# One attention and mixture-of-experts layer on one core: late expert splits moved among the first tiles

## The chip, the cores and the metric

The kernel runs on one core of one Trainium2 chip. The metric is the device time of one execution in microseconds (us); less is better. The core has five engines that work at once and meet by semaphores: TensorE (PE; its weight loads are listed apart as PEld), VectorE (DVE), ScalarE (ACT), GpSimd (POOL) and SyncE (SP), which here only issues DMA. Every engine works through its own instructions in order.

## What is computed

The input `x` is 2 batches of 1024 tokens of 256 numbers. It is normalised (`xn`), and the output is `x + attention(xn) + experts(xn)`, all in float32.

```python
# attention: 16 heads, 4 key/value heads; a semantic part of 32 and a rotated part of 32 per head
k2, v2 = pool(k), pool(v)     # tokens 0..895: means over 14 blocks of 64; tokens 896..1023: as they are
scores = (q_sem @ k_sem2.T + q_geo @ k_geo2.T) / sqrt(32) * exp(logit_scale)
out = softmax(where(k_pos <= pos, scores, NEG_INF)) @ v2 @ Wo
# experts: 16, the best 4 of each token, hidden width 224
g, u = xn @ gate_proj[e], xn @ up_proj[e]
y = sum over the token's 4 experts of top_w * ((silu(g) * u) @ down_proj[e])
```

## The kernel before, in words

The 2048 tokens are 8 tiles of 128 in each of 2 batches (`u`, `b` = 0, 1; tile `t` = 0..7). Only tile 7 sees single keys beside the block means, so its attention is written apart.

**Opening.** `x` is loaded, normalised and turned (`xT`). TensorE projects the rotated keys and the router's logits; VectorE ranks them and takes the best four (L1009 to L1060), and works out the slot of each of the 8192 pairs of token and expert in a list sorted by expert. VectorE also rotates keys (`rope_k`, L991), takes the weights of the four choices one choice at a time (`weights(r)`, L1061), writes the block means of `xn`, the head scales (`hscale`, L1039), and the plan of the tasks (`plan_tasks`, L1102): a task is 128 rows of the sorted list with one expert, `NS` = 79 tasks in all, `tasks` per expert.

**Sending.** GpSimd scatters the rows of `xn` to the list in memory, `xn_by_expert`, in 16 rounds of 4 indirect DMAs (L709 to L720); every round waits until that before it has landed. In the last four rounds it also takes the low parts of experts 4 and 5.

**Splits.** An expert's weights (3 transfers of 224 KB, `load_expert`, L393) are held as a high and a low part, so that three fast products give float32's precision. The high part is two copies on ScalarE (`split_high`, L814: 0.94 and 0.62 us), the low part two subtractions on VectorE (L1192: 1.08 and 0.69 us) or on GpSimd (L687: some 2.1 and 1.3 us). The semaphore `w_hi` counts experts with a high part and `w_lo` those with both, in order, so that each low part waits for the one before it. Experts 0 to 3 (`EARLY` = 4) are loaded in the opening. The others are loaded in groups, `LATE`, with one semaphore a group. SyncE issues group 0 before the loop over blockwise tiles (L615), groups 1 to 3 in turns `i` = 0, 1, 2 of it and groups 4 and 5 later (L623 to L631), group 6 after the first eight tasks (L648). Each turn `i` first stores the sum of tile `i` (`store_sum(i)`, which waits until VectorE has added it, `c_out` >= i + 2), then loads a residual (`load_residual(i + 2)`, which waits until the store before it into that buffer has landed), then the weights.

**Local attention** (tile 7): eight units of one batch and one key/value head. TensorE scores (`l_score`), VectorE takes maxima, ScalarE exponentiates, VectorE divides, TensorE turns (`l_turn`) and multiplies by values (`l_value`); `beside(n)` adds to unit `n` other work: the folded values (`rep_values`, `fold_values`), the tables of the tasks, the first low parts. `l_attend` and `l_attend_blocks` then give the output of tile 7.

**Blockwise attention** (tiles 0 to 6, `attention_pe`, `attention`, `attention_act`). For tile `t` TensorE turns the queries of both batches; then for each batch it projects the queries of tile `t + 1` and scores tile `t`; after the first batch's scores it turns the probabilities of tile `t - 1` (`p_turn`); after both it multiplies those by values (`attend`, L1610), for which it waits for ScalarE's copy of the turned probabilities (`c_pT`). ScalarE in tile `t`: the copies of the queries, the high parts of `SPLITS[t]`'s first expert with their wait, then the copies `p_keep` for tile `t - 1` and the exponentials of tile `t`:

```python
high = SPLITS[t.number]
for k in high[:1]:
    split_late(k)          # waits for w_late of k's group
if not t.first:
    for u in range(NB):
        p_keep(u, t.more(-1))
```

`SPLITS` is written by hand: experts 4, 5 in tile 1; 6, 7 in tile 3; 8, 9 in tile 4; 10 in tile 5. `HEAD` = (11, 12) follows before the first tile of the experts, and `IN_LOOP` = 13: experts 13 to 15 are split in steps 5 to 7 (high) and 6 to 8 (low, on VectorE) of the tiles.

**Tiles of the experts.** 79 tasks, in a software pipeline (`step`): in step `j` TensorE turns the rows of task `j + 2`, multiplies task `j + 1` by gate and up (`three`, six products), turns the activations of task `j` and multiplies those of task `j - 1` by down; ScalarE and VectorE do for each product the copies and subtractions that split it. GpSimd scatters each result into the output, adding to what is there (L741), and begins when its low parts of experts 6 to 12 are done (L723). ScalarE's copy of result `n` waits for scatter `n - 4`. Rows come by `load_task` into 8 slots: SyncE issues tasks 0 to 3 when the rows are sent and tile 6 is scored (L637 to L643), then two stores (the second waits for tile 6's sum), tasks 4 to 7, `load_late(6)`, and then task `j + 8` for each `j`. Steps -2 to 8 are written out, the rest is a loop of 8 steps.

Of the kernel before, what the change touches and what calls it, by code (L numbers as in the profile page):

```python
# [36 lines left out]
P = 128  # L37
# [34 lines left out]
LATE = ((4, 5), (6, 7), (8, 9), (10, 11), (12,), (13,), (14, 15))  # L72
# [20 lines left out]
def build(nc, x, wq_sem, wk_sem, wq_geo, wk_geo, wv, wo, logit_scale, router_w, expert_bias, gate, up, down,  # L93
# [9 lines left out]
    with ctx:  # L103
# [379 lines left out]
        ROUND = 8  # L483

# [48 lines left out]
        def steps(eng, step, rounds, carry=None):  # L533
# [4 lines left out]
            for r in range(-2, ROUND + 1):  # L538
                step(Tile(0, r))
            if carry:  # L540
                carry()
            with eng.Fori(1, rounds) as i:
# [3 lines left out]
                if carry:  # L546
                    carry()
# [5 lines left out]
        def _(sp):  # L553
# [50 lines left out]
            by_batch = vw_d.rearrange("(b r) d -> r b d", b=NB)  # L604
            sp.dma_start(vw[:, :, 0, :], by_batch[0:P, :, :]).then_inc(vw_in, DMA)
# [11 lines left out]
            def load_behind(n, t):  # L617

                for u in range(NB):
                    sp.wait_ge(c_s[u], t)  # L620
                load_late(n)
# [26 lines left out]
            load_late(6)  # L648
# [17 lines left out]
        def _(gp):  # L666
            nc.gpsimd.memset(zero[:, :], 0.0).then_inc(zeros_ready, 1)
            nc.gpsimd.memset(logit[:, :, E:EX], -FAR).then_inc(sentinels_ready, 1)
# [85 lines left out]
        def _(act):  # L754
# [37 lines left out]

            act.wait_ge(pooled, REMOTE)
# [17 lines left out]
            act.wait_ge(vloc_done, 1)  # L811
            nc.scalar.copy(vloc[:, :, :], bank[VLOC_BANK][:, :].rearrange("p (b n) -> p b n", b=NB)).then_inc(vloc_kept, 1)

            def split_high(e):  # L814
                nc.scalar.copy(of_expert(wgu_h, e), of_expert(wgu, e))  # L815
                nc.scalar.copy(of_expert(wdn_h, e), of_expert(wdn, e)).then_inc(w_hi, 1)
# [58 lines left out]
            def split_late(k):  # L875
                if k == SENT:
                    for p in range(GT):
                        act.wait_ge(xs_in[p], K * GROUPS * DMA)
                for n, ks in enumerate(LATE):
# [924 lines left out]
```

## Time and profile before

| | us |
|---|---|
| median of 3 runs (lowest, highest) | 395.76 (393.83, 397.96) |
| the profiled execution, its own time | 395.17 |
| its span, first to last instruction | 393.4 |
| PE busy | 350.6 (89%) |
| DVE busy | 242.4 (62%) |
| POOL busy | 232.0 (59%) |
| ACT busy | 182.6 (46%) |
| mean granted TensorE clock | 0.953 |

The profiled execution took 1.8 us more than its span. Times inside it are us from the span's start. Its stages, by TensorE's work: opening to 59, local attention to 111, blockwise attention to 176, tiles to 384. A granted clock of 1.00 is 2.4 GHz, 0.50 is 1.2 GHz.

### The profile page before, as it was taken

To read this page: it belongs to the slowest core of one execution; us is meant where nothing else is said; L and a number is where in the kernel's file an instruction comes from. 1 tells how busy PE (TensorE), PEld (TensorE's weight loads), DVE (VectorE), ACT (ScalarE), POOL (GpSimd) and SP (SyncE) were. 2 spreads that over 40 slices of the span, in tenths; PEclk is the share of its full clock that TensorE was granted. 3 is DMA by queue.
4 is the path that set the end of the run, shared out by engine and by line. 5 is a ranking of instruction groups with operands and counts; after the bars stand their busy time and mean duration, and the time that the engine had idled before them with its cause. 6 is when DMAs were issued, how large, how long until landed. Compare 5 with 4: busy or idle time off the path is not lost.

```text
span 393.4 us, 8217 instructions
## 1 busy us (share of the span) xinstructions
PE 350.6 (89%) x2085; PEld 287.6 (73%) x2086; DVE 242.4 (62%) x784; ACT 182.6 (46%) x530; POOL 232.0 (59%) x207
## 2 busy tenths in 40 slices
PE   0498997998979999987977999999999999999991
PEld 0393675645746677666876999999999999999881
DVE  3879996488458789852547455555555555555550
ACT  1540186458013344444455455555555555555550
POOL 0600456546664464659987466666666666666664
PEclk9998998699989999996998899999999999999996
DMA  7993112224146388863686476666776766666544
GB/s 247 361 314 89 55 60 84 75 80 125 69 147 209 114 257 257 248 213 86 174 176 100 71 113 107 112 107 107 110 113 108 111 112 112 109 108 107 70 52 53
DMA packets 50094, 52.33 MB, mean 133 GB/s; under 512 B 5632, under 2 KB 47120, under 8 KB 50072
## 3 DMA queue, kind: packets, MB, share of 16 engines
q0 software_dynamic: 14640, 19.34, 29.8%
q1 hardware_dynamic: 35432, 32.73, 29.1%
q8 instruction: 10, 0.16, 0.2%
q14 instruction: 12, 0.10, 0.1%
HBM read 30.14 MB, written 21.91 MB: 132 GB/s over the span
## 4 chain that ended last, share of the span: by engine, by line
PE 48%; DMA 18%; POOL 14%; issue 9%; DVE 6%; ACT 2%; POOLq 1%; SPq 1%; DVEq 0%; ACTq 0%
PE bank L1366 39%; DMA xn_by_expert<-x_all,slot_i 14%; POOL xn_by_expert L714 13%; PE bank L1728 4%; PE bank L1704 4%; DMA out_rows<-y,idx 2%; DMA x_all<-in_L_attn_x 1%; ACT x_all L763 1%; POOL wgu_lo L691 1%; DVE stats L954 1%; PE bank L1378 1%; DVE logit_left L1024 1%; DMA xg<-xn_by_expert 1%; POOLq L103 0%; ACT wgu_hi L815 0%
## 5 line engine op out<-in xcount | busy, mean ns | idle before, releaser
L741 POOL DMA_INDIRECT out_rows<-y,idx x79 | 124.5, 1576 | 66.3 <-ACT y L930 39.6
L714 POOL DMA_INDIRECT xn_by_expert<-x_all,slot_i x64 | 66.2, 1034 | 55.6 <-DMA xn_by_expert<-x_all,slot_i 33.7
L1366 PE MATMUL bank<-wgu_hi,xh 128*128 x158 | 65.9, 417 | 4.7 <-DVE wdn_lo L1195 2.6
L1346 DVE SCALAR_TENSOR_TENSOR act<-bank,xg,sg 128x224 f32<-128x224 f32 x79 | 35.6, 451 | 55.7 <-ACT sg L917 55.7
L1366 PE MATMUL bank<-wgu_lo,xh 128*128 x158 | 59.3, 375 | 0.0
L1366 PE MATMUL bank<-wgu_hi,xl 128*128 x158 | 58.8, 372 | 0.0
L917 ACT ACTIVATE sg<-bank 128x224 f32<-128x224 f32 x79 | 28.3, 358 | 62.3 <-PE bank L1366 62.3
L1338 DVE TENSOR_TENSOR xl<-bank,xh 128x256 fp32r<-128x256 f32 x79 | 33.5, 425 | 35.5 <-ACT xh L908 35.5
L1366 PE MATMUL bank<-wdn_hi,ah 112*128 x158 | 51.8, 328 | 0.6 <-issue 0.5
L1366 PE MATMUL bank<-wdn_hi,al 112*128 x158 | 44.8, 283 | 0.0
L1366 PE MATMUL bank<-wdn_lo,ah 112*128 x158 | 44.6, 282 | 0.0
L930 ACT COPY y<-bank 128x256 f32<-128x256 f32 x79 | 29.5, 374 | 30.6 <-PE bank L1366 27.4
L1366 PEld LDWEIGHTS bank<-wgu_hi,xh 128*128 128x128 f32 x158 | 30.4, 192 | 7.3 <-issue 5.2
L1704 PE MATMUL bank<-const_k,xg 128*128 128x128 f32 x158 | 31.2, 279 | 4.6 <-DMA xg<-xn_by_expert 4.6
L908 ACT CAST xh<-bank 128x256 fp32r<-128x256 f32 x79 | 29.8, 378 | 7.4 <-PE bank L1704 7.0
L1354 DVE TENSOR_TENSOR al<-bank,ah 112x256 fp32r<-112x256 f32 x79 | 32.8, 415 | 0.5 <-ACT ah L921 0.5
L1366 PEld LDWEIGHTS bank<-wgu_hi,xl 128*128 128x128 f32 x158 | 30.4, 192 | 2.8
L1366 PE MATMUL bank<-wqg,xT 128*128 128x512 f32 x64 | 32.1, 628 | 0.0
L1366 PEld LDWEIGHTS bank<-wgu_lo,xh 128*128 128x128 f32 x158 | 30.6, 194 | 1.2
L1366 PEld LDWEIGHTS bank<-wdn_hi,ah 112*128 112x128 f32 x158 | 30.3, 192 | 1.2 <-issue 1.0
L1728 PE MATMUL bank<-const_k,act 128*112 128x128 f32 x158 | 30.6, 275 | 0.0
L1366 PEld LDWEIGHTS bank<-wdn_lo,ah 112*128 112x128 f32 x158 | 30.4, 193 | 0.0
(235 smaller groups left out, 658.2 us busy)
## 6 DMA issues: line engine op xcount, KB each, us to landing
xg<-xn_by_expert SPq DMA_DIRECT2D x79, 129.0 KB, 2.5
wgu<-in_L_ffn_gate_proj SPq DMA_DIRECT2D x16, 224.0 KB, 4.0
wgu<-in_L_ffn_up_proj SPq DMA_DIRECT2D x16, 224.0 KB, 4.6
wdn<-in_L_ffn_down_proj SPq DMA_DIRECT2D x16, 224.0 KB, 4.9
x_all<-in_L_attn_x SPq DMA_DIRECT2D x8, 256.0 KB, 5.0
xr<-in_L_attn_x SPq DMA_DIRECT2D x14, 128.0 KB, 2.2
out_rows<-xr SPq DMA_DIRECT2D x14, 128.0 KB, 3.8
out_rows<-y,idx POOLq DMA_INDIRECT x79, 3.8
```

Of the source, the lines that this page charges most:

```text
L691: nc.gpsimd.tensor_tensor(of_expert(wgu_l, e), of_expert(wgu, e), of_expert(wgu_h, e).bitcast(F32), ALU.subtract)
L714: gp.indirect_dma_start(xs_d, bass.IndirectOffsetOnAxis(slot_i[:, z, r:r + 1], 0), x_all[:, z, :], None).then_inc(xs_in[p], DMA)
L741: gp.indirect_dma_start(out_rows, bass.IndirectOffsetOnAxis(idx[r % RING][:, 0:1], 0), ysb[r % 4][:, :], None, compute_op=ALU.add).then_in ...
L908: nc.scalar.copy(xh[t.par][:, :, :], bank[t.par][:, 0:D].rearrange("p (c n) -> p c n", c=DC)).then_inc(xh_ready, 1)
L917: nc.scalar.activation(sg[t.par][:, :], bank[2 + t.par][:, 0:I], ACT.Silu).then_inc(sg_ready, 1)
L930: nc.scalar.copy(ysb[t.place][:, :], bank[6 + t.par][:, 0:D]).then_inc(y_ready, 1)
L1338: nc.vector.tensor_tensor(xl[t.par][:, :, :], bank[t.par][:, 0:D].rearrange("p (c n) -> p c n", c=DC), xh[t.par][:, :, :].bitcast(F32), AL ...
L1346: nc.vector.scalar_tensor_tensor(av[t.par][:, :], bank[2 + t.par][:, I:2 * I], xg[t.slot][:, D + 1:D + 2], sg[t.par][:, :], ALU.mult, ALU. ...
L1354: nc.vector.tensor_tensor(al[t.par][:, :, :], bank[4 + t.par][0:IH, 0:2 * P].rearrange("p (c n) -> p c n", c=2), ah[t.par][:, :, :].bitcas ...
L1366: return nc.tensor.matmul(o, lhsT, rhs, start=start, stop=stop)
L1704: last = nc.tensor.transpose(bank[t.par][:, c * P:(c + 1) * P], xg[t.slot][:, c * P:(c + 1) * P], ident)
L1728: last = nc.tensor.transpose(bank[4 + t.par][0:IH, c * P:(c + 1) * P], av[t.par][:, c * IH:(c + 1) * IH], ident)
```

## The change

Constants and the order of the splits. Groups 4 and 5 of one expert each become one of two; ScalarE has experts 4 and 5 in tile 1, 6 and 7 in tile 3, 8 and 9 in tile 5 of the attention, none ahead of the tiles, and 10 to 15 in steps 2 to 13 of the tiles, one of an expert's two copies in each step; VectorE has their low parts in steps 4 to 15, one subtraction in each. GpSimd's loop ends with expert 9. Steps -2 to 16 of the tiles are written out (`HEAD = 2 * ROUND`), and the loop has one turn less.

```diff
-LATE = ((4, 5), (6, 7), (8, 9), (10, 11), (12,), (13,), (14, 15))
+LATE = ((4, 5), (6, 7), (8, 9), (10, 11), (12, 13), (14, 15))
-        SPLITS = ((), (4, 5), (), (6, 7), (8, 9), (10,), ())
-        HEAD = (11, 12)
+        SPLITS = ((), (4, 5), (), (6, 7), (), (8, 9), ())
-        IN_LOOP = 13
+        IN_LOOP = 10
+        HIGH_FROM, LOW_FROM = 2, 4
...
         def _(act):
...
                     for u in range(NB):
                         p_keep(u, Pair(0, REMOTE - 1))
-                    for k in HEAD:
-                        split_late(k)
...
-                if j.counts is None and j.r in (5, 6, 7):
-                    split_late(IN_LOOP + j.r - 5)
+                n = j.r - HIGH_FROM
+                if j.counts is None and 0 <= n < 2 * (E - IN_LOOP):
+                    split_late(IN_LOOP + n // 2, (n % 2,))
...
         def _(dve):
...
-                if j.counts is None and j.r in (6, 7, 8):
-                    k = IN_LOOP + j.r - 6
-                    dve.wait_ge(w_lo, k)
-                    split_low(k)
+                n = j.r - LOW_FROM
+                if j.counts is None and 0 <= n < 2 * (E - IN_LOOP):
+                    k = IN_LOOP + n // 2
+                    if n % 2 == 0:
+                        dve.wait_ge(w_lo, k)
+                    split_low_part(k, n % 2)
```

SyncE's loads: groups 1 and 2 in turns 1 and 3, group 3 after tasks 0 to 3, groups 4 and 5 after tasks 4 to 7.

```diff
             for i in range(REMOTE - 3):
                 store_sum(i)
                 load_residual(i + 2)
-                if i < 3:
-                    load_late(i + 1)
-                else:
-                    load_behind(4, 2)
+                if i % 2:
+                    load_late(i // 2 + 1)
             store_sum(REMOTE - 3)
-            load_behind(5, 4)
...
             for j in range(RING // 2):
                 load_task(j, j)
+            load_late(3)
             for i in range(REMOTE - 2, REMOTE):
                 store_sum(i)
             for j in range(RING // 2, RING):
                 load_task(j, j)
-            load_late(6)
+            load_late(4)
+            load_late(5)
```

A task for every expert, in `plan_tasks`:

```diff
                 link(nc.vector.tensor_tensor(tasks[:, :], tiles_f[:, :], bound[:, 1, :], ALU.subtract))
+                link(nc.vector.tensor_scalar(tasks[:, :], tasks[:, :], 1.0, None, ALU.max))
```

Opening and local attention. On VectorE the four operations that make the weights' sums and the three of the head scales move behind the rotation of keys 2 and 3 and the slots (the scales behind all keys), the fold of the block means (`x_fold`) in front of `weights(1)`, and `weights(2)` and `weights(3)` into units 2 and 6 of the local attention. On TensorE the local values (`vloc`, from `xT[REMOTE]` now) come right after the rotated queries of tile 7, and ScalarE's copy of them ahead of its others; the folded values come before the first turn:

```diff
             l_score(0)
             l_score(1)
+            rep_values()
             for n in range(UNITS):
                 l_turn(n)
...
             l_attend(0)
             l_value(UNITS - 1)
-            q_project(0, Pair(0, 0))
+            for u in range(NB):
+                q_project(u, Pair(0, 0))
...
             turn_probabilities(1)
-            q_project(1, Pair(0, 0))
             l_attend_blocks(1)
```

VectorE accordingly does `rope(u, Pair(0, 0))` for both batches, then `split_low(3)` and `keep_before()`, then `l_attended(u)`, each followed by a new `memset` of `prT[u]`.

128 rows in the values' products: `attend` takes all 128 rows of every chunk in place of the 32 to 128 that hold probabilities. The new memset of `prT`, and one of `vw[:, :, 1, :]` on GpSimd at the start, make the rest zero.

```diff
-                parts = [(prT[u][0:rest, n, :], vw[0:rest, u, n, :]) for n, (at, rest) in enumerate(t.chunks)]
+                parts = [(prT[u][:, n, :], vw[:, u, n, :]) for n in range(len(t.chunks))]
```

## Rows read from the trace of the kernel before

**Rows 1.** Windows of ten us: busy (x instructions) by engine, granted clock, DMA share, GB/s.
```profile
70.00:80.00 10.00, 10.00 (x43) 5.43 (x44) 6.07 (x26) 4.55 (x13) 4.67 (x6) 0.68 0.18 64
...
150.00:160.00 10.00, 10.00 (x54) 7.05 (x53) 9.00 (x27) 5.39 (x12) 4.64 (x6) 1.00 0.83 255
...
250.00:260.00 10.00, 10.00 (x70) 9.28 (x69) 5.65 (x19) 5.20 (x17) 6.50 (x5) 1.00 0.69 112
```

**Rows 2.** The chain that ended last, where the tiles begin: start, us, what.
```profile
170.33 5.13 DMA xn_by_expert<-x_all,slot_i
177.71 2.11 DMA xg<-xn_by_expert
```

**Rows 3.** Timeline of ScalarE (ACT), blockwise attention: start, us, engine, line, operation [idle before <-releaser].
```profile
144.48 0.94 ACT L815 CAST wgu_hi<-wgu 128x896 fp32r<-128x896 f32 x1 [2.22 <-DMA wdn<-in_L_ffn_down_proj]
...
154.20 0.94 ACT L815 CAST wgu_hi<-wgu 128x896 fp32r<-128x896 f32 x1 [3.48 <-DMA wdn<-in_L_ffn_down_proj]
...
155.56 0.42 ACT L872 COPY prT<-bank 128x128 f32<-128x128 f32 x2
...
163.88 0.94 ACT L815 CAST wgu_hi<-wgu 128x896 fp32r<-128x896 f32 x1 [4.73 <-DMA wdn<-in_L_ffn_down_proj]
```

**Rows 4.** Timeline of SyncE's DMA issues, blockwise attention.
```profile
131.66 1.47 SPq L588 DMA_DIRECT2D out_rows<-xr  x2
135.51 1.03 SPq L583 DMA_DIRECT2D xr<-in_L_attn_x  x2
...
141.47 0.89 SPq L588 DMA_DIRECT2D out_rows<-xr  x2
145.47 0.81 SPq L583 DMA_DIRECT2D xr<-in_L_attn_x  x2
146.33 0.43 SPq L400 DMA_DIRECT2D wgu<-in_L_ffn_gate_proj  x1
```

**Rows 5.** Timeline of TensorE (PE), blockwise attention and the first transpose of the tiles.
```profile
147.83 1.11 PE L1366 MATMUL bank<-vw,prT 96*128 96x256 f32 x4
...
165.71 2.58 PE L1366 MATMUL bank<-vw,prT 128*128 128x256 f32 x8 [0.38 <-ACT prT L872]
...
178.72 0.66 PE L1704 MATMUL bank<-const_k,xg 128*128 128x128 f32 x2 [3.19 <-DMA xg<-xn_by_expert]
```

**Rows 6.** Timeline of TensorE, local attention and the change to blockwise.
```profile
64.49 0.66 PE L1506 MATMUL bank<-const_k,lex 128*128 128x128 f32 x4 [2.06 <-DVE lex L1184]
...
66.81 3.62 PE L1366 MATMUL bank<-x_fold,wv_rep 128*128 128x30 f32 x16
...
113.98 3.53 PE L1366 MATMUL bank<-wqg,xT 128*128 128x512 f32 x4
```

**Rows 7.** Timeline of TensorE, the first gate product of five of the tiles.
```profile
191.71 0.46 PE L1366 MATMUL bank<-wgu_hi,xh 128*128 x1
...
206.06 0.74 PE L1366 MATMUL bank<-wgu_hi,xh 128*128 x1 [2.18 <-DVE xl L1338]
...
215.18 0.47 PE L1366 MATMUL bank<-wgu_hi,xh 128*128 x1 [2.56 <-DVE wdn_lo L1195]
...
221.52 0.45 PE L1366 MATMUL bank<-wgu_hi,xh 128*128 x1
...
223.91 0.45 PE L1366 MATMUL bank<-wgu_hi,xh 128*128 x1
```

**Rows 8.** Timeline of ScalarE, fifth step of the tiles.
```profile
203.34 0.37 ACT L930 COPY y<-bank 128x256 f32<-128x256 f32 x1 [2.33 <-DMA out_rows<-y,idx]
```

**Rows 9.** Timeline of GpSimd (POOL), its first output scatter.
```profile
199.20 1.62 POOL L741 DMA_INDIRECT out_rows<-y,idx  x1 [0.16 <-issue]
```

**Rows 10.** Timeline of SyncE's DMA issues, first tiles.
```profile
191.70 0.44 SPq L400 DMA_DIRECT2D wgu<-in_L_ffn_gate_proj  x1
...
195.84 4.35 SPq L635 DMA_DIRECT2D xg<-xn_by_expert  x4
```

**Rows 11.** Tile `xg`, 186 to 206 us: time to landing.
```profile
DMA to landing us min/median/max: 2.1/2.6/4.4
```

More of the change, by code:

```diff
@@ L483, in build @@
         ROUND = 8
+        HEAD = 2 * ROUND
         class Tile:
@@ L533, in steps @@
         def steps(eng, step, rounds, carry=None):
-            for r in range(-2, ROUND + 1):
+            for r in range(-2, HEAD + 1):
                 step(Tile(0, r))
             if carry:
-                carry()
-            with eng.Fori(1, rounds) as i:
+                carry(HEAD)
+            with eng.Fori(HEAD // ROUND, rounds) as i:
                 counts = Counts(eng, ROUND, i), Counts(eng, ROUND // 4, i, True), Counts(eng, ROUND // RING, i, True)
@@ L810, in _, with split_high_part @@
                 keep_rep(n)
-            act.wait_ge(vloc_done, 1)
-            nc.scalar.copy(vloc[:, :, :], bank[VLOC_BANK][:, :].rearrange("p (b n) -> p b n", b=NB)).then_inc(vloc_kept, 1)
+            def split_high_part(e, part):
+                if part == 0:
+                    nc.scalar.copy(of_expert(wgu_h, e), of_expert(wgu, e))
+                else:
+                    nc.scalar.copy(of_expert(wdn_h, e), of_expert(wdn, e)).then_inc(w_hi, 1)
             def split_high(e):
-                nc.scalar.copy(of_expert(wgu_h, e), of_expert(wgu, e))
-                nc.scalar.copy(of_expert(wdn_h, e), of_expert(wdn, e)).then_inc(w_hi, 1)
+                for part in range(2):
+                    split_high_part(e, part)
             def l_exp(n):
@@ L873, in p_keep, with split_late @@
                 last.then_inc(c_pT[u], 1)
[L875 to L879, printed above, removed]
-                    if k == ks[0]:
-                        act.wait_ge(w_late[n], len(ks) * 3 * DMA)
-                split_high(k)
+            def split_late(k, parts=(0, 1)):
+                if 0 in parts:
+                    if k == SENT:
+                        for p in range(GT):
+                            act.wait_ge(xs_in[p], K * GROUPS * DMA)
+                    for n, ks in enumerate(LATE):
+                        if k == ks[0]:
+                            act.wait_ge(w_late[n], len(ks) * 3 * DMA)
+                for part in parts:
+                    split_high_part(k, part)
             def attention_act(t):
@@ L1329, in _ @@
             for u in range(NB):
+                rope(u, Pair(0, 0))
+            split_low(3)
+            keep_before()
+            for u in range(NB):
                 l_attended(u)
-                rope(u, Pair(0, 0))
+                link(nc.vector.memset(prT[u][:, :, :], 0.0))
             pairs(attention)
@@ L1438, in _ @@
                 last.then_inc(l_q, 1)
+            pe.wait_ge(kv_in, 4 * DMA)
+            pe.wait_ge(slots_ready, 1)
+            for b in range(NB):
+                for c in range(DC):
+                    last = mm(bank[VLOC_BANK][:, b * D:(b + 1) * D], xT[REMOTE][:, b, c, :], wv_s[:, c, :], c == 0, c == DC - 1)
+            last.then_inc(vloc_done, 1)
             for t in range(4, REMOTE):
@@ L1473, in _ @@
                 rep_keys(n)
-            pe.wait_ge(slots_ready, 1)
-            for b in range(NB):
-                for c in range(DC):
-                    last = mm(bank[VLOC_BANK][:, b * D:(b + 1) * D], x_keys[:, c, b, NBLK:NKEY], wv_s[:, c, :], c == 0, c == DC - 1)
-            last.then_inc(vloc_done, 1)
             def l_score(n):
@@ L1543, in beside @@
                 if n == 0:
-                    rep_values()
                     pe.wait_ge(starts_ready, 1)
@@ L1645, in _ @@
             l_value(UNITS - 1)
-            q_project(0, Pair(0, 0))
+            for u in range(NB):
+                q_project(u, Pair(0, 0))
             pe.wait_ge(asem_kept, DC)
@@ L1711, in step @@
                     e = expert(t)
-                    if t.counts is None and t.r <= ROUND + 1:
+                    if t.counts is None and t.r <= HEAD + 1:
                         pe.wait_ge(w_lo, pe.to_reg(e + 1))
```

61 lines of the change are left out of this document (33 added, 28 removed).

## The prediction

> **What bounds the kernel now.** I read the windows of ten us first. Inside the blockwise attention TensorE is busy all of its time, as in the steady tiles [rows 1], so a stage is as long as TensorE's work plus what stops it. The places to look for are those where TensorE stands still or has the low clock. The timelines show four. (a) In the local attention it waits 2.06 us for VectorE before the first turn, and in the next window, 70 to 80, its clock is 0.68, that is 1.2 GHz for most of it [rows 1, 6]. (b) Between local and blockwise attention it waits for VectorE's rotation, and the projection at 113.98 takes 3.53 us, where its like at 2.4 GHz take 1.9 [rows 6]. (c) The chain of waits runs through the scatters of `xn_by_expert` until 175.5 and the first load of a tile; TensorE's first transpose comes at 178.72 after 3.19 idle, again at the low clock [rows 2, 5]. (d) The first gate product of tile 3 is at 191.71, that of tile 12 at 221.52, 29.8 us for nine tiles; the steady distance is 223.91 - 221.52 = 2.39, so nine should take 21.5. The 8.3 us between are three things: GpSimd begins to scatter only at 199.20, because seven experts' low parts come first, so ScalarE's copy of a result waits 2.33 us for a scatter [rows 8, 9]; the splits of experts 13 to 15 then stop TensorE for 2.18 and 2.56 us; and the clock falls after each [rows 7].
>
> The profiled execution took 395.17 us, 0.6 below the median of 395.76; my sum is made against it.
>
> **Opening: -0 to -1 us, taken with the next part.** Keys in front of weights frees TensorE some two us earlier, but VectorE does the same work in another order and its rotation of tile 7's queries ends where it did. The one operation more in `plan_tasks` (0.2 us) has no wait behind it. `weights(2)` and `weights(3)` go into units 2 and 6, before GpSimd's rounds 8 and 12 want them. The early memset on GpSimd lies in the wait for inputs.
>
> **Local attention: -5.5 us (-2 to -7.5).** `rep_values` took 3.62 us at the low clock [rows 6]; at the high clock I take 2.1 (half, and a little). It now fills the 2.06 of idle time, so the low end of the gain is 2. If the clock also stays up, the ten us of slow work after 66 shrink by up to five more. Against this: the local values leave their place ahead of the first score, where ScalarE's copies of the keys are what is waited for, so there TensorE waits two us more, and the clock may fall there instead. Between the ends I take the middle and a little, 5.5.
>
> **Change to blockwise: -2.0 us (-1 to -3.5).** With both first projections and rotations done beside the tile-7 output, the wait for the second rotation goes, and with it the low clock: 3.53 - 1.9 = 1.6, plus 1.5 of waiting, less about one us because `l_attend_blocks(1)` now follows its own copy on ScalarE with nothing between. The memsets of `prT` (estimated at 0.3 us each) lie on VectorE beside TensorE's projections.
>
> **Loads in turns 1 and 3: +16.0 us (+10.5 to +19), and +4.5 us of clock (+2 to +6).** This decides the sign. Before, the weights issued in turn `i` are split in tile `i + 3`, and already then ScalarE waits for them: 2.22, 3.48 and 4.73 us [rows 3]. Now experts 6 and 7 are issued in turn 1 and still split in tile 3, and 8 and 9 in turn 3 and split in tile 5: one tile later against their use, and a tile is over eight us. In the profile of before: turn 1 begins with its store at 141.47, goes on when that store has landed at 145.47, issues the weights from 146.33 [rows 4], and the wait for them ends at 154.20 [rows 3], 7.9 us after the first issue. ScalarE reaches the wait of tile 3 at 144.48 - 2.22 = 142.26. It will wait 11.9 us instead of 2.2, and then split expert 6 (1.36 us until the next instruction, 155.56 - 154.20) before the copies of `prT`, the second of which is there at some 155.8. TensorE's `attend` in tile 3 was at 147.83 with no wait [rows 5]: it now stops for 155.8 - 147.8 = 8.0. Queued behind ScalarE's wait are those copies, both exponentials of tile 3 and expert 7; behind TensorE's wait the turned queries of tile 4, and so every later tile. In tile 5 the same, at `attend` of 165.71: the wait there ends with a group loaded one turn later than that of 163.88, so +9.5 by the rows, less some two us because SyncE has no weights ahead of that store: 8. Lower bound for each: a store takes 135.51 - 131.66 = 3.85 when no weights are beside it [rows 4], so only the weights' own 7.9 us can shrink; if by a third, the two stops are 5.3 each, 10.5 together. Upper: 9.5 each. After idle times of 2 to 3 us TensorE worked at 1.2 GHz for 3 to 7 us (the product at 206.06 takes 0.74 where that at 221.52 takes 0.45 [rows 7]); half of that time is lost, so 2.2 each.
>
> Blockwise attention then ends 16 + 4.5 - 7.5 = 13 us later. The rounds of GpSimd will end a few us earlier for want of weights beside them (six experts in place of ten), but that no longer matters: the scatters were last by 2 to 3 us, and are now done before the attention.
>
> **Start of the tiles: -4.3 us (-2 to -5.5).** With the rows sent early, SyncE issues the first loads when tile 6 is scored, 3 us earlier against the attention, and the load lies beside TensorE's last `attend`. The idle 3.19 us shrinks to about half a us and the slow work after it runs at 2.4 GHz; from both I count 4.3. Group 3, put behind tasks 0 to 3, is six issues of 0.5 us, which lie in SyncE's wait for tile 6's sum. `HEAD`'s two splits (2.7 us on ScalarE) go, but lay beside TensorE's slow products.
>
> **Ramp of the tiles: -8.3 us (-6.5 to -8.3).** GpSimd has four low parts of 3.3 us and is done long before the first result, so the wait on a scatter goes. One copy of 0.84 us net on ScalarE and one subtraction of 1.0 us net on VectorE a step fit: their four operations a step take about 1.1 to 1.2 of 2.39 us. TensorE does not wait for experts 10 to 15: tile 16 is still expert 3 or 4.
>
> **Tile 8 behind the weights: +5.5 us (+1 to +12).** Groups 4 and 5, twelve transfers, now go out from where `load_late(6)` began, 191.70 [rows 10], right ahead of task 8. Before there were six, task 8 was issued at 195.84, and the slowest load of a tile took 4.4 us [rows 10, 11]: it landed near 200.2, just in time for its transpose at some 201.1. Twelve transfers take 6 us to issue and, at 7.9 us for six and 4.5 for each six more, are down at 204; that is a stop of 3 us. The scatters of results now run beside them, which none of before's loads shows; if they take half of the DMA engines, the stop is 10. I take 4, nearest to the row, and 1.5 for the clock; with both ends the term is 1 to 12.
>
> **128 rows** in the values' products: a product of 96 rows takes 1.11 us for four and one of 128 rows 2.58 for eight [rows 5], so rows cost little or nothing: 0 (-0.5 to +0.3). The longer written-out part and one turn less of the loop: 0 (+-0.5).
>
> **Sum.** -5.5 - 2.0 + 16.0 + 4.5 - 4.3 - 8.3 + 5.5 = +5.9, less the half us of the opening: +5.4. 395.17 + 5.4 = **400.6 us**, 1.2% above the median.
>
> **Rivals.**
> A, *the weights come sooner* (faster): with fewer groups in the queue a group needs 5.3 us instead of 7.9, and twelve do not hold up task 8. Then the stops are 10.5, their clock 3, tile 8 costs 1: -0.5 - 5.5 - 2 + 10.5 + 3 - 4.3 - 8.3 + 1 = -6.1, **389 us**. It decides once a group lands within some 6 us of its first issue; for it speaks that the three waits grew with the traffic (2.2, 3.5, 4.7), against it that the first, with only scatters beside it, also took 7.9 (issued at 136.6, waited for until 144.48).
> B, *the scatters of results and the weights share the DMA engines*: tile 8 costs 12 instead of 5.5: **407 us**. The Trainium skill ("DMA: Bandwidth & Descriptors", "Queues, rings and completion order") says that an engine takes turns between the queues with work, a packet from each; by that rule the scatters slow the weights, and task 8 in their queue with them.
> C, *the wait on ScalarE stays hidden*: the splits' waits of before cost TensorE 0.38 us in all [rows 5]. If the new ones were hidden too, attention would end 7.5 earlier, the scatters would set the start at about -4, and the sum is -4 - 8.3 + 5.5: **388 us**. Against it: the 2 us of slack between the copies and `attend` are smaller than the wait that is added.
> D, *the clock falls in the local attention again* and the gain there is 2: **404 us**.
>
> **How the numbers follow.** Forecast 0.42, A 0.16, B 0.16, C 0.08, D 0.18. Under 1% (4 us) is about what a measurement of this kernel can't tell from no change. The forecast lies at that edge and its terms add up to some +-4, so half of it goes to slower, a third to same; B and D are slower; A and C faster but for a rest. That makes faster 0.24, same 0.22, slower 0.54. The range of 8 in 10 goes from 388 to 408: A just inside, B inside, and one in ten left on each side. The likeliest case's own range is 397 to 405.
>
> **What would show it.** ScalarE's first high part in tiles 3 and 5 waits 10 to 12 us for a weight's DMA, and TensorE's product `vw, prT` after it 7 to 9 us for `prT`. No wait of `xn_by_expert` stands last at the start of the tiles. ScalarE's copy of a result no longer waits for a scatter in the first steps; from tile 3 gate products come every 2.4 us, but for one gap of 3 us or more before tile 8, with the transpose waiting for `xg`. I am wrong if TensorE stays busy through the blockwise attention, or if the gap at tile 8 is missing and the stops are below 5 us.

## The result, and the profile after

The changed kernel takes 398.84 us (median of 20 runs, 395.37 to 402.75) against 395.1 us for the kernel before on the same chips (20 runs, 389.35 to 399.66). The ratio is 1.0128, 95% interval 1.0091 to 1.0165: slower by 1.3%. Every ratio here is taken over the fast runs alone (those within 1.5% of the fastest of their kernel), so it can differ from the quotient of the medians given beside it. The profiled execution took 400.72 us (span 398.8, mean granted clock 0.957), against 395.17 (span 393.4) before.

The forecast was 400.6, "slower". The two profiled executions differ by 5.5 us, the medians by 3.7. I cut both profiles at six instructions of TensorE that exist in both and read the differences; everything below refers to this table (us from the span's start; the last column is the length of the stretch that ends there, after minus before).

| point on TensorE | before | after | stretch |
|---|---|---|---|
| first local score | 59.37 | 59.96 | +0.6 |
| last turn of local probabilities | 95.77 | 92.60 | -3.8 |
| query turn of tile 1 (of blockwise) | 121.66 | 115.93 | -2.6 |
| values' products in tile 6 | 173.00 | 181.64 | +14.4 |
| first gate product of tile 3 (of the experts) | 191.71 | 198.05 | -2.3 |
| the same of tile 12 | 221.52 | 226.86 | -1.0 |
| end of the span | 393.4 | 398.8 | 0.1 |

The sum is +5.4. After tile 12 the two kernels are equal.

**The stops in the blockwise attention.** The timeline of ScalarE in the changed kernel, where [rows 3] stood:

```profile
146.64 0.94 ACT L812 CAST wgu_hi<-wgu 128x896 fp32r<-128x896 f32 x1 [10.89 <-DMA wdn<-in_L_ffn_down_proj]
...
148.00 0.42 ACT L874 COPY prT<-bank 96x128 f32<-96x128 f32 x2
...
171.84 0.94 ACT L812 CAST wgu_hi<-wgu 128x896 fp32r<-128x896 f32 x1 [10.07 <-DMA wdn<-in_L_ffn_down_proj]
...
173.21 0.72 ACT L874 COPY prT<-bank 128x128 f32<-128x128 f32 x4
```

Each wait for a weight's transfer stands in the brackets ahead of the split (`wgu_hi`), and the copy of `prT`, for which TensorE waits, is queued right behind it. On TensorE, where [rows 5] stood:

```profile
148.31 2.08 PE L1380 MATMUL bank<-vw,prT 128*128 128x256 f32 x4 [6.98 <-ACT prT L874]
150.18 1.91 PE L1477 MATMUL bank<-const_k,q 128*128 128x128 f32 x8
...
173.67 3.41 PE L1380 MATMUL bank<-vw,prT 128*128 128x256 f32 x8 [5.71 <-ACT prT L874]
176.91 1.04 PE L1477 MATMUL bank<-const_k,q 128*128 128x128 f32 x8
...
185.27 0.41 PE L1719 MATMUL bank<-const_k,xg 128*128 128x128 f32 x2 [1.67 <-DMA xg<-xn_by_expert]
186.19 0.44 PE L1719 MATMUL bank<-const_k,xg 128*128 128x128 f32 x2 [0.52 <-DMA xg<-xn_by_expert]
```

TensorE stands still for 6.98 and 5.71 us, and the turn of queries behind the first stop takes 1.91 us, behind the second 1.04: that is how the two levels of the clock look. Why the groups come late is in SyncE's issues:

```profile
135.06 0.82 SPq L589 DMA_DIRECT2D out_rows<-xr  x2
136.80 1.12 SPq L584 DMA_DIRECT2D xr<-in_L_attn_x  x2
137.98 0.43 SPq L400 DMA_DIRECT2D wgu<-in_L_ffn_gate_proj  x1
...
140.63 0.47 SPq L402 DMA_DIRECT2D wdn<-in_L_ffn_down_proj  x1
...
161.14 0.83 SPq L589 DMA_DIRECT2D out_rows<-xr  x2
163.06 0.82 SPq L584 DMA_DIRECT2D xr<-in_L_attn_x  x2
163.92 0.43 SPq L400 DMA_DIRECT2D wgu<-in_L_ffn_gate_proj  x1
```

The first issue of the group is at 137.98 and ScalarE's wait ends at 146.64: 8.7 us; the other group, issued from 163.92, has 7.9.

**The tiles.** First gate products and the transposes that waited, where [rows 7] stood:

```profile
197.74 0.44 PE L1719 MATMUL bank<-const_k,xg 128*128 128x128 f32 x2 [2.08 <-DMA xg<-xn_by_expert]
198.05 0.47 PE L1380 MATMUL bank<-wgu_hi,xh 128*128 x1
...
200.45 0.45 PE L1380 MATMUL bank<-wgu_hi,xh 128*128 x1
...
202.83 0.45 PE L1380 MATMUL bank<-wgu_hi,xh 128*128 x1
...
205.22 0.45 PE L1380 MATMUL bank<-wgu_hi,xh 128*128 x1
...
212.45 0.69 PE L1719 MATMUL bank<-const_k,xg 128*128 128x128 f32 x2 [4.84 <-DMA xg<-xn_by_expert]
212.79 0.72 PE L1380 MATMUL bank<-wgu_hi,xh 128*128 x1
...
217.17 0.61 PE L1380 MATMUL bank<-wgu_hi,xh 128*128 x1
...
219.72 0.45 PE L1380 MATMUL bank<-wgu_hi,xh 128*128 x1
```

From tile 3 on the products come every 2.39 us, without the waits of [rows 7] and [rows 8]; then task 8's transpose waits 4.84 us for its load, and tile 7's gate product, queued behind it, runs at 0.72 us instead of 0.45. The granted clock of the stretches (the columns are those of [rows 1]):

```profile
60.00:64.00 4.00, 4.00 (x18) 2.08 (x20) 0.81 (x2) 0.73 (x5) 1.62 (x3) 0.57 0.18 66
64.00:70.00 6.00, 6.00 (x46) 4.27 (x42) 3.66 (x11) 4.42 (x18) 4.26 (x5) 1.00 0.25 88
...
146.00:153.00 7.00, 4.69 (x14) 3.64 (x15) 2.35 (x8) 4.72 (x10) 4.08 (x5) 0.52 0.27 96
...
170.00:177.00 7.00, 3.33 (x9) 2.69 (x10) 0.91 (x2) 3.96 (x10) 5.17 (x4) 0.53 0.19 65
177.00:186.00 9.00, 7.00 (x49) 6.05 (x47) 6.07 (x18) 4.27 (x11) 9.00 (x6) 1.00 0.19 59
211.00:218.00 7.00, 5.55 (x21) 5.14 (x22) 2.33 (x5) 1.98 (x5) 0.00 (x0) 0.53 0.58 149
```

1.00 is 2.4 GHz, 0.50 is 1.2 GHz: the low clock lies behind each stop, and in the first local scores.

### The profile page after: what moved, and what is told of

Same layout as the page of the kernel before. It is cut to its first block, busy times and chain, and to the rows that moved or that the text cites. A ratio compares the mean times of both kernels' runs of the same rounds, so it can differ in the third digit from the quotient of the medians.

```text
span 398.8 us, 8176 instructions
## 1 busy us (share of the span) xinstructions
PE 344.1 (86%) x2085; PEld 286.4 (72%) x2086; DVE 247.3 (62%) x793; ACT 182.6 (46%) x530; POOL 221.3 (55%) x202
## 4 chain that ended last, share of the span: by engine, by line
PE 61%; DVE 14%; DMA 9%; SPq 6%; issue 5%; ACT 4%; POOLq 1%; DVEq 0%
PE bank L1380 50%; PE bank L1719 4%; PE bank L1743 4%; DMA wdn<-in_L_ffn_down_proj 3%; DMA xg<-xn_by_expert 2%; DMA x_all<-in_L_attn_x 1%; PE bank L1477 1%; DMA out_rows<-xr 1%; DVE x_keys L1090 1%; DVE lneg L1174 1%; SPq L401 1%; ACT x_all L760 1%; SPq L400 1%; DVE lex L1184 1%; DVE q L1081 1%
## 5 line engine op out<-in xcount | busy, mean ns | idle before, releaser
L738 POOL DMA_INDIRECT out_rows<-y,idx x79 | 123.2, 1560 | 86.0 <-ACT y L932 50.1
L912 ACT CAST xh<-bank 128x256 fp32r<-128x256 f32 x79 | 29.8, 377 | 10.5 <-PE bank L1719 10.2
L1380 PE MATMUL bank<-wqg,xT 128*128 128x512 f32 x64 | 30.5, 603 | 0.0
```

The source lines that it names most:

```text
L738: gp.indirect_dma_start(out_rows, bass.IndirectOffsetOnAxis(idx[r % RING][:, 0:1], 0), ysb[r % 4][:, :], None, compute_op=ALU.add).then_in ...
L912: nc.scalar.copy(xh[t.par][:, :, :], bank[t.par][:, 0:D].rearrange("p (c n) -> p c n", c=DC)).then_inc(xh_ready, 1)
L1380: return nc.tensor.matmul(o, lhsT, rhs, start=start, stop=stop)
```

## The experiments

All are timed beside the kernel before (medians of 395.2 to 396.2 us). The changed kernel was not timed again beside them; its 398.84 us is that of the result.

**1. The groups one turn earlier** (turn_earlier):

```diff
-                if i % 2:
+                if i % 2 == 0:
                     load_late(i // 2 + 1)
```

> The changed kernel, with experts 6 and 7 issued in turn 0 and 8 and 9 in turn 2 in place of turns 1 and 3. My theory (the two stops come from the turn in which a group is issued): ScalarE's waits for weights in tiles 3 and 5 fall from 10.9 and 10.1 us to 2 to 4, TensorE's stops of 7.0 and 5.7 us before the values' products to under 1 each, and the attention ends 14 to 16 us earlier. The scatters of xn_by_expert, which end at 172.9 in the changed kernel, are then last at the start of the tiles again, so that only 8 to 11 us reach the end: 388 to 391 us. Rival (the groups need as long wherever they are issued, and slow the scatters, since they run beside them): the scatters end 4 us or more later, 394 to 397 us. Rival (the stop is the copy's and not the group's): no change, 399 us.

Measured 390.21 us (ratio to before 0.989, 0.9842 to 0.9937). ScalarE's waits in tiles 3 and 5 are 2.45 and 1.48 us, no values' product waits for `prT` any more, and the stretch from tile 1's query turn to the products of tile 6 takes 49.1 us in place of 65.7. The first transpose of the tiles then waits:

```profile
174.35 0.66 PE L1719 MATMUL bank<-const_k,xg 128*128 128x128 f32 x2 [7.78 <-DMA xg<-xn_by_expert]
...
201.78 0.69 PE L1719 MATMUL bank<-const_k,xg 128*128 128x128 f32 x2 [6.06 <-DMA xg<-xn_by_expert]
```

The attention ends 17 us earlier, and 7.78 us of it are spent waiting for the scatters: GpSimd's own wait for the last of them ends at 171.52. The clock is low behind that wait too (the first transposes take 0.66 us). The theory holds, both rivals fall.

**2. Experts 14 and 15 behind tasks 8 to 11** (group5_behind):

```diff
             load_late(4)
-            load_late(5)
...
+            for j in range(RING):
+                load_next(j, j, lambda v: v)
+                if j == 3:
+                    load_late(5)
-            with sp.Fori(0, LAPS) as i:
+            with sp.Fori(1, LAPS) as i:
```

> The changed kernel, with experts 14 and 15 issued behind tasks 8 to 11 in place of ahead of task 8 (so the loads of the first eight tasks after the ring stand in code of their own ahead of the loop). My theory (task 8 is late because twelve transfers stand in its queue): the stop of 4.84 us before the transposes of task 8 falls to under 1.5 us, the clock does not fall there, and the kernel is 4 to 7 us faster than the changed one: 392 to 395 us. Rival (the scatters of results take the DMA engines from every load, in whatever place): the stop stays over 3 us, or comes back at task 12, and the time is within 2 us of 399.

Measured 392.5 us (0.9972, 0.9933 to 1.001), 6.3 below the changed kernel. From tile 3 to tile 12 (194.61 to 216.06) it is 21.45 us, nine times 2.38: no stop.

```profile
58.00:64.00 6.00, 4.96 (x36) 3.48 (x36) 2.62 (x7) 3.29 (x17) 3.02 (x5) 1.00 0.18 66
206.00:212.00 6.00, 6.00 (x43) 5.65 (x41) 5.34 (x14) 4.78 (x14) 4.11 (x3) 1.00 1.11 278
```

Between 206 and 212 the DMA engines are as loaded as ever (share 1.11, 278 GB/s) with scatters of results and weights at once, and TensorE does not notice. So with twelve transfers ahead of it in its queue task 8 stops TensorE, with six it doesn't, at this load on the engines: rival B of the prediction falls. The page of the Trainium skill that I had cited for it ("DMA: Bandwidth & Descriptors", "Queues, rings and completion order") says that an engine takes turns between queues; the trace doesn't speak against that, but it decided nothing here.

**3. Both** (both):

> The changed kernel with both edits: experts 6 to 9 issued one turn earlier each, 14 and 15 behind tasks 8 to 11. My theory, in which the two are independent: the sum of the two gains, 382 to 387 us, faster than the kernel before by 2 to 3 per cent. Rival (the start of the tiles is set by the scatters, and with it the tables, the stores and the loads crowd there): less than the sum, 387 to 392 us.

Measured 381.87 us (0.9695, 0.9646 to 0.9743): 17.0 below the changed kernel where the single gains add up to 8.6 + 6.3 = 14.9, and 3% faster than the kernel before. The idle time ahead of the first load is 8.17 us here, so the rival's crowding is there too, but it had been there in run 1 and isn't counted twice.

**4. 32, 64 and 96 rows again** (rows96, and the same kernel a second time, rows96_again):

```diff
-                parts = [(prT[u][:, n, :], vw[:, u, n, :]) for n in range(len(t.chunks))]
+                parts = [(prT[u][0:rest, n, :], vw[0:rest, u, n, :]) for n, (at, rest) in enumerate(t.chunks)]
```

> The changed kernel with the values' products of the second chunk on 96 rows again, as before the change. My theory (rows of a product cost nothing, only columns do): 398 to 400 us, within 0.5 of the changed kernel, and the eight products take 2.5 to 2.7 us in the tiles with the high clock. Rival (the rows count): 1 us or more faster, from 28 products of 256 columns.

> The changed kernel with 32, 64 and 96 rows in the values' products a second time, since its first run was 7 us above the changed kernel where none was expected. Theory (few rows let the clock fall or keep it down): again 403 us or more, with the clock low behind tile 0 or for over 10 us behind the stop in tile 5. Rival (which of the marginal falls comes is chance from one loading of the program to the next): anything from 397 to 406 us, and the low stretches elsewhere than in the first profile.

Measured 406.33 and 405.74 us (1.0281, 1.0216 to 1.0345; 1.0346, 1.0256 to 1.0435): 7 us above the changed kernel, twice. A part of it is the products themselves (experiment 5 shows how much), the rest is the clock. TensorE of rows96, with no idle time ahead of any of these:

```profile
123.63 0.69 PE L1380 MATMUL bank<-vw,prT 32*128 32x256 f32 x2
124.26 0.70 PE L1380 MATMUL bank<-vw,const_k 104*128 104x256 f32 x2
124.89 0.69 PE L1380 MATMUL bank<-vw,prT 32*128 32x256 f32 x2
125.51 1.19 PE L1380 MATMUL bank<-vw,const_k 104*128 104x256 f32 x2
126.49 1.91 PE L1477 MATMUL bank<-const_k,q 128*128 128x128 f32 x8
```

The fourth pair takes 1.19 us where the second took 0.70, and the turn of queries 1.91 where it takes 1.04 in the changed kernel: the clock fell in the middle of gapless work. This fall wasn't there in the second profile (124 to 130 has 1.00), nor in the profiles of the kernel before and of experiment 5, which have the same products on 32 rows. What both profiles have is the slow recovery behind the stop in tile 5. The windows of rows96, of rows96_again, and of the changed kernel:

```profile
172.00:190.00 18.00, 12.54 (x41) 9.20 (x41) 3.95 (x12) 6.27 (x17) 13.10 (x8) 0.54 0.19 62
```
```profile
176.00:184.00 8.00, 8.00 (x32) 6.18 (x32) 2.64 (x9) 1.42 (x5) 8.00 (x6) 0.55 0.09 33
```
```profile
176.00:184.00 8.00, 7.59 (x50) 6.66 (x48) 4.73 (x15) 3.40 (x9) 8.00 (x6) 0.96 0.10 33
```

Behind about the same stop, 176 to 184 has 0.55 with few rows and 0.96 with 128. From tile 1's turn to the products of tile 6 the two profiles take 75.3 and 69.8 us, the changed kernel 65.7: +9.6 and +4.1. Three further profiles have these two stops and 128 rows (group5_behind, and rep_back and vloc_front below). Without the stops themselves the stretch takes 53.0 to 54.6 us in the four profiles with 128 rows, and 61.5 and 57.3 in the two with few.

**5. The same step where nothing stops** (both_rows96, experiment 3 with the rows of experiment 4) **and the reverse in the kernel before** (before_rows128, whose edit is shown; SyncE also waits for the cleared part of `vw`):

```diff
+            nc.gpsimd.memset(vw[:, :, 1, :], 0.0).then_inc(zeros_ready, 1)
...
                 l_attended(u)
+                link(nc.vector.memset(prT[u][:, :, :], 0.0))
...
-                parts = [(prT[u][0:rest, n, :], vw[0:rest, u, n, :]) for n, (at, rest) in enumerate(t.chunks)]
+                parts = [(prT[u][:, n, :], vw[:, u, n, :]) for n in range(len(t.chunks))]
```

> The kernel with both edits of the loads (382 us), with the values' products on 32, 64 and 96 rows again. In the changed kernel that step back cost 7 us where I had expected none: the products take the same time (0.69 us for two, 1.11 for four), but the granted clock fell at 125.5, right behind the 32-row products of tile 0, with no idle time before it, and after the stop at 171 it stayed low until 189 in place of some 175. Theory (few rows at a time let the clock fall or keep it down): the clock falls behind tile 0 again, tile 1 is 2 us later, but the attention has no stops and ends with 8 us of slack before the first load of a tile, so that 0 to 2 us reach the end: 382 to 384 us. Rival (the 7 us were bad luck of that kernel's places and not of its rows): clock 1.00 from 120 to 165 and 381 to 382 us.

> The kernel before with the 128 rows alone: the second part of vw and both prT cleared once, all values' products on 128 rows. In the trace of before the clock is 1.00 from 120 to 170, beside products of 32, 64 and 96 rows, so my theory of the prediction (no cost, no gain) gives 394.5 to 396. The theory from the run with fewer rows (few rows let the clock fall) allows a gain only where the clock was low, behind the last tiles of the attention and at the start of the tiles: up to 2 us, 393 to 395.

Measured 383.43 us (0.9711, 0.9643 to 0.978) beside the 381.87 of experiment 3, and 397.14 (1.0019, 0.9968 to 1.007). Neither difference can be told from none, and in neither profile is the clock low between tile 1 and the end of the attention. The fall behind tile 0 that I expected of the first did not come. But the rows are hidden here, not free. Two groups of eight products, all at 2.4 GHz, first in both, then in both_rows96, where half of the first group are on 32 rows and half of the second on 64:

```profile
157.41 1.96 PE L1383 MATMUL bank<-vw,prT 128*128 128x256 f32 x8
...
163.93 1.95 PE L1383 MATMUL bank<-vw,prT 128*128 128x256 f32 x8
```
```profile
156.11 2.54 PE L1383 MATMUL bank<-vw,prT 128*128 128x256 f32 x8
...
163.37 2.54 PE L1383 MATMUL bank<-vw,prT 128*128 128x256 f32 x8
```

Tile 0's four pairs take 2.41 us on 32 rows and 1.81 on 128. From tile 1's turn to the products of tile 6 it is 50.8 us against 49.1, without a stop in either: 1.7 us of TensorE's time, and 0.6 more for the products at the end. They don't reach the end of the kernel, because the first load of a tile is waited for 8.52 and 8.17 us behind them. In before_rows128 the two groups take 1.99 us each where the kernel before takes 2.58 and 2.54, but TensorE then waits 1.11, 1.46 and 0.30 us for `prT` behind ScalarE's waits for weights, where it waited 0.38 before. Of the 7 us of experiment 4, then, an estimated 2.3 are the products; what is left is mostly the clock behind the stops.

**6. The products of folded x at three places.** Behind the first turn, as before (rep_back: `rep_values()` goes from its line behind `l_score(1)` into `beside(0)`); ahead of the scores, in the kernel of experiment 3 (rep_first, in which they also wait until ScalarE has copied what was in their bank, `rep_kept`):

```diff
-            l_score(0)
-            l_score(1)
-            rep_values()
+            rep_values()
+            l_score(0)
+            l_score(1)
```

> The changed kernel with the products of folded x and wv_rep behind the first turn again. My step (they fill the wait before the first turn, 2.1 us, and keep the clock up): that wait of 2 us comes back, the clock falls behind it, and the local attention is 2 to 5 us longer: 401 to 404 us. Rival (the clock falls at 60 us in any case, so it is up again by the first turn): 2 us or less, 399 to 401 us.

> The kernel with both edits of the loads (382 us), with the products of folded x and wv_rep ahead of the first score, in TensorE's wait of 2.4 us for ScalarE's copies, in place of behind the second. Theory (the clock that falls at 60 us is from that wait): TensorE does not stand still there, the first scores run at 2.4 GHz, and the first turn comes at some 65 in place of 66.5; the wait for VectorE ahead of the first turn comes back with up to 2 us. Since the scatters of xn_by_expert set the start of the tiles, and they hang on VectorE's and GpSimd's work and not on this, 0 to -2 us reach the end: 380 to 382 us. Rival (the work at 57 to 62 only moves, and the clock falls before the first turn, as in the kernel before): 382 to 384 us.

rep_back: 403.38 us (1.024, 1.0168 to 1.0312), 4.5 above the changed kernel; first score to last turn takes 38.4 us in place of 32.6, with the 2.06 us of idle time and the 3.62 us at the low clock of [rows 6] back to the hundredth. rep_first: 382.65 (0.9679, 0.9615 to 0.9744), no gain over 381.87; the clock is 1.00 at 60, falls at 66 behind the wait for VectorE (2.06 us), and the stretch takes 33.2 us. Its rival was right: the fall only moves. (In the profile of rep_back the clock did not fall at 60, so the stretches differ by more than the medians.)

**7. The local values' products ahead of the first score** (vloc_front), with ScalarE's copy of them back in its old place too:

```diff
-                    last = mm(bank[VLOC_BANK][:, b * D:(b + 1) * D], xT[REMOTE][:, b, c, :], wv_s[:, c, :], c == 0, c == DC - 1)
...
             for n in range(HKV, 2 * HKV):
                 rep_keys(n)
+            pe.wait_ge(slots_ready, 1)
+            for b in range(NB):
+                for c in range(DC):
+                    last = mm(bank[VLOC_BANK][:, b * D:(b + 1) * D], x_keys[:, c, b, NBLK:NKEY], wv_s[:, c, :], c == 0, c == DC - 1)
```

> The changed kernel with the local values' products where they were before: behind the products of the keys, ahead of the first score. There they fill most of TensorE's wait of 2.37 us for ScalarE's copies (0.65 us of it was left in the kernel before), while the products of folded x and wv_rep go on filling the wait ahead of the first turn. In the profiles so far, all with the same code up to here, the clock fell behind the wait of 2.37 us in five and stayed up in two, and those two reach the blockwise attention 1 to 3 us earlier. Theory (that wait decides whether the clock falls): no fall between 58 and 70 us, the last turn at 90 or before in place of 92.6, and 1 to 3 us less in the median: 396 to 398 us. Rival (the work left out at 47 us lets the clock fall somewhere else): 399 us or more.

Measured 400.83 us (1.0192, 1.0107 to 1.0277): not faster. The clock did stay up (the window 58 to 64 has 1.00, and so has 64 to 70), but the stretch takes 32.4 us all the same: counted from the first score the second turn comes 1.4 us before that of the changed kernel, the third, which waits 1.13 us for VectorE, only 0.3. The theory fell. (It also miscounted: by the profiles up to then the clock had fallen in four and stayed up in three.) Where the clock stays up in the kernel without this move, the stretch takes 30.8 to 31.9 us, so the move itself costs about what it gives in this stretch.

**8. Rounds of scatters that overlap** (overlap, in all rounds; overlap_late, in rounds 9 to 15 only), on top of experiment 3. The second part of the edit is that of overlap_late; in overlap every round waits for the round before:

```diff
-                    gp.indirect_dma_start(xs_d, bass.IndirectOffsetOnAxis(slot_i[:, z, r:r + 1], 0), x_all[:, z, :], None).then_inc(xs_in[p], DMA)
+                    gp.indirect_dma_start(xs_d, bass.IndirectOffsetOnAxis(slot_i[:, z, r:r + 1], 0), x_all[:, z, :], None).then_inc(xs_in[n % 2 * GT + p], DMA)
...
+                m = n if n < 9 else n - 1
                 for p in range(GT):
-                    gp.wait_ge(xs_in[p], (n + 1) * DMA)
+                    gp.wait_ge(xs_in[m % 2 * GT + p], (m // 2 + 1) * DMA)
```

> The kernel with both edits of the loads (382 us), in which GpSimd waits, behind each round of four scatters of xn_by_expert, for the round before it and no longer for that round itself (two sets of semaphores, taken in turns). In the trace of the 382 us kernel TensorE stands still for 8.2 us ahead of the first load of a tile, and a round takes four issues of 1.28 us and a wait of 2.2 to 5.3 us for its landing. Theory (the rounds' waits set the start of the tiles): the waits go, the last scatter lands 10 us or more earlier, and then TensorE's attention is last: its idle time falls under 2 us and the clock stays up, 370 to 376 us. Rival (the scatters share the DMA engines with the weights and only the load on them counts): the last scatter lands 0 to 3 us earlier, or the weights for tiles 1, 3 and 5 land later and stop ScalarE: 379 to 384 us.

> The kernel with both edits of the loads (382 us), in which rounds 0 to 8 of the scatters wait for themselves as before, and rounds 9 to 15, which lie beside the change to blockwise attention and the attention itself, wait for the round before. The run that did this for all rounds lost some 24 us in the local attention, in waits that the trace gives to no engine, and nothing beside the blockwise attention. Theory (the scatters alone hold the start of the tiles, and beside the blockwise attention they may overlap): the last scatter lands before 160 in place of 170.4, the idle 8.2 us ahead of the first load of a tile fall under 2.5, and the low clock behind them goes: 371 to 376 us. Rival (the unexplained waits follow the overlap wherever it is): 383 us or more. Rival (the tiles' tables or the stores are last just behind the scatters): 377 to 381 us.

overlap: 398.4 us (1.0156, 1.0069 to 1.0242), 16.5 us lost. ScalarE and VectorE, and TensorE with them, stand still in the local attention, in waits to which the trace gives no engine (`remote`). ScalarE:

```profile
52.64 0.59 ACT L802 COPY qsT<-bank 128x512 f32<-128x512 f32 x1 [6.16 <-remote]
57.03 0.17 ACT L805 COPY kgeo_t<-bank 128x14 f32<-128x14 f32 x1 [3.81 <-remote]
...
60.01 0.89 ACT L792 ACTIVATE rep_s<-bank,slot_scale 128x284 f32<-128x284 f32 x2 [2.40 <-remote]
...
86.09 0.58 ACT L842 COPY lpT<-bank 128x512 f32<-128x512 f32 x1 [5.79 <-remote]
```

overlap_late: 381.24 us (0.9653, 0.9607 to 0.9698), within the spread of experiment 3. What the theory and what its first rival describe both happened, and all but cancelled: GpSimd's wait for the last scatter ends at 159.5 in place of 171.2, TensorE waits 1.61 us instead of 8.17 for the first load, but the attention's end is 4.3 us later (168.20 against 163.93), with the same waits in it:

```profile
120.85 0.26 ACT L880 COPY prT<-bank 32x128 f32<-32x128 f32 x1 [2.37 <-remote]
...
128.92 0.59 ACT L897 COPY qrT<-bank 128x512 f32<-128x512 f32 x1 [2.92 <-remote]
...
134.19 0.42 ACT L880 COPY prT<-bank 64x128 f32<-64x128 f32 x2 [2.48 <-remote]
```

The profiles of turn_earlier and both have no wait of this kind on ScalarE between 50 and 130 us. What these waits are stays open. It is not the load on the DMA engines alone: their share is 0.27 from 50 to 64 us in overlap, less than in many stretches where nothing waits.

## Why the prediction was right, and where it wasn't

**Loads in turns 1 and 3: right in place, mechanism and sign.** I took 8 + 8 us of stops and 4.5 of clock; measured 7.0 + 5.7, less the 0.4 of before, and 14.4 - 12.3 = 2.1 of clock. The stops are smaller because the stores landed sooner than the 3.85 us I took from [rows 4]: SyncE goes on 1.7 and 1.9 us after them (135.06 to 136.80, 161.14 to 163.06). So my lower bound had it the wrong way round: it held the store fixed and let the weights shrink. The weights themselves took 8.7 and 7.9 us, against 7.9 in the working. The 2.1 is not the clock alone, since the 128 rows take some 1.7 us off the same stretch (experiment 5): the clock cost some 3.8 of the 4.5. Experiment 1 shows that the turn of issue is the whole cause of the two stops. Rival A falls with the 8.7 and 7.9 us that a group took, C with TensorE's stops.

**128 rows: the step that failed.** I put the term at 0 (-0.5 to +0.3) from a misread row. The 2.58 us for eight products in [rows 5] are not eight on 128 rows: the merged line names one shape only, four of them are on 32 rows, and eight on 128 take 1.96 (experiment 5). Beside the 1.11 us of four products on 96 rows the row seemed to say that few rows cost nothing; on 32 and 64 rows they do. The step is worth 2.3 us of TensorE's time up to the end of the attention (experiment 5), 1.7 of them hidden in the +14.4 and 0.6 in the start of the tiles. It is worth more behind a stop: taken back, the kernel loses 7 us (experiment 4), most of them because the clock comes back later. The sum had no term for that. In the kernel before, the time that it saves goes into waits for weights.

**Local attention: -5.5 forecast, -3.8 measured** (with the 0.6 by which the opening is later, -3.2). Rival D's mechanism is there: the wait ahead of the first score grew from 0.65 to 2.37 us, and the clock fell behind it. In three profiles with the same code here and no fall (group5_behind, both_rows96, overlap_late) the stretch takes 30.8, 30.9 and 31.9 us against 36.4 before, a gain of 4.5 to 5.6. So the 5.5 was right for a local attention without the fall. Experiment 6 confirms the rest, 4.5 us for the place of `rep_values`. **Change to blockwise: -2.0 forecast, -2.6 measured**; the projection at 109.89 takes 1.88 us, at the high clock.

**Start of the tiles: -4.3 forecast, -2.3 measured.** The idle time shrank from 3.19 to 1.67 + 0.52 us, not to half a us, and the clock fell again (0.72 for the first gate product at 186.84). I had put the load beside TensorE's last products; but SyncE sends it at 183.02, 1.4 us after they begin (181.64), and it takes 2.2 us where they take 1.95. And the wait for task 4's rows, ahead of tile 3's product, grew from 0.97 us (the row below, from the kernel before) to 2.08 (at 197.74): tasks 4 to 7 are issued from 193.32, behind two stores that need tile 6's sum.

```profile
191.40 0.44 PE L1704 MATMUL bank<-const_k,xg 128*128 128x128 f32 x2 [0.97 <-DMA xg<-xn_by_expert]
```

**Ramp: -8.3 forecast, exactly so.** Tile 3 to tile 12 takes 28.8 us, 7.3 of them at task 8; experiment 2 without that stop takes 21.45 against 29.8. **Task 8: +5.5 forecast, +7.3 measured**, 4.84 of stop and 2.5 of clock. Its load was issued at 205.35, behind the twelve transfers, and landed some 15 us after the first of them was issued at 197.06, where I had twelve down in 12.4 (7.9 and 4.5; no row shown gives the 4.5). The slowest load took 7.2 us in place of 4.4 [rows 11].

So the terms are -3.2, -2.6, +14.4, -2.3, -8.3, +7.3, which give +5.3, against -6.0, -2.0, +20.5, -4.3, -8.3, +5.5, which give +5.4. The total is better than its parts: the gains up to tile 3 were overrated by 4.2 us, the stops by 6.1, and task 8 was 1.8 short. That the sum came out to the tenth of a us is luck: the errors cancel, the profile of the changed kernel happens to have the fall at 60 us that four of nine profiles lack, and the medians differ by 3.7 us and not by 5.4.

## What to carry to other kernels

When a load moves from one iteration to another, count the iterations between issue and use on both sides before anything else; here one turn was worth 8.6 us, and the way back was one line. A transfer that everybody waits for must not stand behind twelve that nobody needs yet. And a fix far from the end pays only up to the next thing in line: the idle 7.8 us behind experiment 1, and experiment 8, show what the rest of it is worth. And an edit that leaves the total as it was may still save or cost time that a later wait hides: compare the same instructions at the same clock before calling it free.

## What the runs showed of the hardware that I had not expected

- **Behind the same wait the clock falls in one profile and not in the next.** Nine of these profiles have the same code up to the first local score and the same wait of 2.37 us ahead of it. In five (first score at 59.34 to 60.07) the clock fell behind it, in four (58.37 to 58.94) it stayed at 1.00. The two sets lie 0.4 us apart; that the moment decides it was not tested. A difference of 1 to 2 us between two profiles in this stretch says nothing of an edit elsewhere.
- **Products on few rows are not free.** At 2.4 GHz eight products of 256 columns take 1.95 us on 128 rows and 2.54 when four of them are on 32 or 64. Four on 96 rows take the 1.11 us of four on 128, and eight of which four are on 96 rows the 1.89 of eight on 128 (rows96, vloc_front).
- **Behind one of two stops the clock stayed low longer with few rows.** Behind the stop in tile 5 it was back 3 to 6 us after TensorE went on in the four profiles with 128 rows, and 9 and 13 us after in the two with few. Behind the stop in tile 3, with products on 96 rows, there is no difference: 4 and 5 us against 3 to 5. Why was not shown.
- **Scatters of GpSimd that overlap delay instructions of other engines**, by up to 6 us at a time, also at a DMA share of 0.27. The cause wasn't found; in this kernel it ate the whole gain.
